# Laying x out by partition, loading it in eight groups, splitting the first piece of the adjacency matrix, and moving two waits to their first reader

## What is computed

```python
dn = de = diag(adj)
A  = adj with its diagonal set to zero
node_support = A @ h                                    # h is x
edge_output  = gru(node_support, h, edge weights)
for each of 3 heads:                                    # W is 128 x 128, a is 256 x 1
    hW = h @ W
    hp, hm = (A > 0) @ hW, (A < 0) @ hW
    e_plus  = leaky_relu([hp, hm] @ a);  e_minus = leaky_relu([hm, hp] @ a)
    att = softmax over a row of (e_plus where A > 0, e_minus where A < 0)
    edge_support += (att * A) @ hW
node_output = gru(edge_support / 3, h, node weights)
x = layernorm(x + de * edge_output + dn * node_output)
# second layer: a graph convolution with tanh(adj * adj), keeping 350 a row
x = layernorm(x + relu(new_adj @ (tanh(x @ W_proj + b) @ W_gcn) + b2))
```

## Time and profile before

| | us |
|---|---|
| median of three runs | 1399.0 (1397.55 to 1399.67) |
| the profiled execution, whole | 1400.07 |
| its span, first to last instruction | 1398.3 |
| TensorE busy in the span | 1349.2 (96%) |
| VectorE busy | 1027.8 (74%) |
| ScalarE busy | 960.9 (69%) |
| mean granted TensorE clock | 0.981 of full speed |

### The profile page before, as it was taken

One profiled execution on the slowest core, in us unless ns is written; L12 is line 12 of the kernel. 1 busy time (PEld: TensorE's weight loads), 2 busy tenths in 40 slices (PEclk: granted clock), 3 DMA queues, 4 the chain that ended last, 5 costly groups with the idle time before them and its releaser, 6 DMA issues.

```text
span 1398.3 us, 11293 instructions
## 1 busy us (share of the span) xinstructions
PE 1349.2 (96%) x3716; PEld 627.6 (45%) x3716; DVE 1027.8 (74%) x1327; ACT 960.9 (69%) x1086; POOL 88.6 (6%) x188
## 2 busy tenths in 40 slices
PE   7999999989999999999999999999997889999996
PEld 3544444355444444444444444444443444444455
DVE  3244333436699998999989999899957885678883
ACT  4355445317688988889888898898935654556663
POOL 0000001000010010100100100101002430000000
PEclk9899999999999999999999999999999989999998
DMA  9687888244324242242323324223062006888860
GB/s 365 248 281 270 283 281 272 109 108 159 136 91 145 84 150 103 92 164 91 136 90 121 136 90 153 104 90 121 0 280 96 30 16 213 300 299 302 301 222 17
DMA packets 49321, 228.91 MB, mean 164 GB/s; under 512 B 10536, under 2 KB 20456, under 8 KB 23528
## 3 DMA queue, kind: packets, MB, share of 16 engines
q1 hardware_dynamic: 46688, 225.55, 46.1%
q10 hardware_dynamic: 2568, 2.58, 0.5%
HBM read 223.82 MB, written 4.29 MB: 163 GB/s over the span
## 4 chain that ended last, share of the span: by engine, by line
PE 67%; DVE 6%; POOL 3%; issue 1%; ACT 1%; DMA 1%; SPq 0%; POOLq 0%; DVEq 0%
PE t_y_ps L1689 46%; PE t_y_ps L1262 11%; PE t_y_ps L1667 4%; PE rows_ps L1262 2%; DVE mask L1140 2%; PE t_es_ps L1660 1%; DMA pieces<-scratch_ns_t 1%; PE t_y_ps L1213 1%; ACT pieces L1007 1%; POOL h_newton L960 1%; POOL h_newton L956 1%; POOL h_newton L958 1%; POOL h_root L962 1%; PE t_y_ps L1215 0%; DVE x_sb L1121 0%
## 5 line engine op out<-in xcount | busy, mean ns | idle before, releaser
L1689 PE MATMUL t_y_ps<-mask,x_sb 128*128 128x512 f32 x1536 | 663.0, 592 | 0.3 <-DVE mask L1607 0.3
L1689 PEld LDWEIGHTS t_y_ps<-mask,x_sb 128*128 128x128 f32 x1536 | 290.1, 190 | 364.0 <-issue 342.9
L1607 DVE TENSOR_TENSOR mask<-mask 128x1536 f32<-128x1536 f32 x256 | 449.0, 1755 | 2.0 <-ACT mask L1491 2.0
L1491 ACT ACTIVATE mask<-mask,ones 128x1536 f32<-128x1536 f32 x256 | 399.7, 1562 | 0.0
L1484 ACT ACTIVATE mask<-mask,pieces 128x512 f32<-128x512 f32 x352 | 241.3, 712 | 31.7 <-PE t_y_ps L1689 28.4
L383 PE MATMUL ns_ps<-pieces,x_sb 128*128 128x512 f32 x512 | 232.2, 609 | 10.0 <-DMA pieces<-in_adj_c 7.7
L1593 DVE TENSOR_SCALAR mask<-mask,e_cols 128x512 f32<-128x512 f32 x416 | 188.1, 484 | 56.7 <-PE t_y_ps L1689 45.7
L1262 PE MATMUL t_y_ps<-mask 128*128 128x512 f32 (+1 forms) x448 | 182.1, 565 | 0.0
L383 PEld LDWEIGHTS ns_ps<-pieces,x_sb 128*128 128x128 f32 x512 | 96.9, 194 | 133.1 <-issue 132.6
L210 ACT ACTIVATE signs<-pieces 128x2048 fp8e4<-128x2048 f32 x64 | 122.3, 1911 | 30.9 <-DMA pieces<-in_adj_c 15.7
L1140 DVE SCALAR_TENSOR_TENSOR mask<-mask 128x2048 f32<-128x2048 f32 x64 | 142.7, 2284 | 0.0
(11 more groups left out here) (163 smaller groups left out, 662.8 us busy)
## 6 DMA issues: line engine op xcount, KB each, us to landing
mask<-in_adj_c SPq DMA_DIRECT2D x128, 1024.0 KB, 4.8
pieces<-in_adj_c SPq DMA_DIRECT2D x64, 1024.0 KB, 4.9
mask<-scratch_shifts SPq DMA_DIRECT2D x8, 1536.0 KB, 7.7
mask<-in_x_t SPq DMA_DIRECT2D x1, 2048.0 KB, 16.4
scratch_ns_t<-ns_sb ACTq DMA_DIRECT2D x8, 256.0 KB, 5.9
pieces<-in_x_t SPq DMA_DIRECT2D x8, 256.0 KB, 2.9
pieces<-scratch_ns_t SPq DMA_DIRECT2D x8, 256.0 KB, 3.9
out<-x_sb SPq DMA_DIRECT2D x7, 256.0 KB, 6.4
```

The lines of the kernel that those rows point to most:

```text
L1491: nc.scalar.activation(t, t, ACT.Exp, bias=ones[:, :], scale=-1.0).then_inc(exped, 1)
L1607: nc.vector.tensor_tensor(term(n), term(n), a, ALU.mult).then_inc(terms, 1)
L1689: mm = nc.tensor.matmul(y_ps[c % 2][h][:, :], x_sb[:, k, :], term(n)[:, h, :], start=k == 0, stop=k == NB - 1)
```

## The change

x is laid out ahead of the launch as in_x_p, [128, 32, 128], so that each partition's 32 tiles are next to each other and a group of four tiles is 2 KB. It is loaded in eight transfers of 256 KB, each issued just ahead of the piece that uses it (for n from 5 on behind the three waits of that piece), and each with a semaphore of its own. Piece 0 is loaded in four transfers of 256 KB (one tile for each partition, 2 KB next to each other), each with a semaphore, and TensorE waits for each just ahead of the matmul that reads it; VectorE and ScalarE wait for all four. The wait for `split` moves from the start of chunk 1 to pos_products(0), and the wait for `const_ready` to sum_e(0). Loads of slot 0 are counted one less (loads_of), since piece 0 no longer counts there. in_x goes.

```diff
--- before.py
+++ after.py
@@ -82,17 +82,21 @@
     engine.dma_start(pieces[:, n % RING, :, :], dram["adj_c"][c, :, g * PIECE:(g + 1) * PIECE, :]).then_inc(loaded[n % RING], 16)
 
 
+def loads_of(n):
+
+
+    return 16 * (n // RING + (1 if n % RING else 0))
+
+
 def wait_piece(engine, loaded, cleared, n):
 
     c, g = piece_of(n)
     if g == c:
         engine.wait_ge(cleared, CHUNK * (c + 1))
     else:
-        engine.wait_ge(loaded[n % RING], 16 * (n // RING + 1))
-
-
-X_SINGLE = 4
-X_REST = (slice((X_SINGLE + 1) * PIECE, NB), slice(0, PIECE))
+        engine.wait_ge(loaded[n % RING], loads_of(n))
+
+
 UV_AFTER = NPIECE - 1
 MASKS_FIRST = UV_AFTER + 3
 LAST_EARLY = 4
@@ -128,9 +132,10 @@
 
 
     w_ready, x_t_ready, const_ready = sem("a_w"), sem("a_x_t"), sem("a_const")
-    x_ready = [sem(f"a_x{n}") for n in range(X_SINGLE + 1)]
+    x_ready = [sem(f"a_x{n}") for n in range(NPIECE)]
     exps, parts_made, small = sem("a_exps"), sem("a_parts"), sem("a_small")
     loaded = [sem(f"a_loaded{s}") for s in range(RING)]
+    first_loaded = [sem(f"a_first_loaded{j}") for j in range(PIECE)]
     folded, folded_out, uv_done, uv_out, split = (sem("a_" + n) for n in ("folded", "folded_out", "uv_done", "uv_out", "split"))
     filled, cleared, masked, signed, ns_done, ns_out, pos_done, prod_out = (
         sem("a_" + n) for n in ("filled", "cleared", "masked", "signed", "ns_done", "ns_out", "pos_done", "prod_out"))
@@ -172,22 +177,25 @@
 
         @block.sync
         def _(sp):
-            x_rows = dram["x"].rearrange("(t p) f -> p t f", p=P)
-            for n in range(X_SINGLE):
-                tiles = slice((n + 1) * PIECE, (n + 2) * PIECE)
-                sp.dma_start(x_sb[:, tiles, :], x_rows[:, tiles, :]).then_inc(x_ready[n], 16)
-                load_piece(sp, dram, pieces, loaded, n)
-            for tiles in X_REST:
-                sp.dma_start(x_sb[:, tiles, :], x_rows[:, tiles, :]).then_inc(x_ready[X_SINGLE], 16)
-            for n in range(X_SINGLE, RING):
-                load_piece(sp, dram, pieces, loaded, n)
-            for n in range(RING, NPIECES):
+            for n in range(NPIECE):
+                tiles = slice((n + 1) % NPIECE * PIECE, ((n + 1) % NPIECE + 1) * PIECE)
+                if n >= RING:
+                    sp.wait_ge(masked, n - RING + 1)
+                    sp.wait_ge(signed, n - RING + 1)
+                    sp.wait_ge(ns_done, n - RING + 1)
+                sp.dma_start(x_sb[:, tiles, :], dram["x_p"][:, tiles, :]).then_inc(x_ready[n], 16)
+                if n:
+                    load_piece(sp, dram, pieces, loaded, n)
+                else:
+                    for j in range(PIECE):
+                        sp.dma_start(pieces[:, 0, j, :], dram["adj_c"][0, :, PIECE + j, :]).then_inc(first_loaded[j], 16)
+                if n == UV_AFTER:
+                    sp.dma_start(x_t, dram["x_t"]).then_inc(x_t_ready, 16)
+            for n in range(NPIECE, NPIECES):
                 sp.wait_ge(masked, n - RING + 1)
                 sp.wait_ge(signed, n - RING + 1)
                 sp.wait_ge(ns_done, n - RING + 1)
                 load_piece(sp, dram, pieces, loaded, n)
-                if n == UV_AFTER:
-                    sp.dma_start(x_t, dram["x_t"]).then_inc(x_t_ready, 16)
 
         @block.gpsimd
         def _(pool):
@@ -196,7 +204,7 @@
                 c, g = piece_of(n)
                 if g != c:
                     continue
-                pool.wait_ge(loaded[n % RING], 16 * (n // RING + 1))
+                pool.wait_ge(loaded[n % RING], loads_of(n))
                 for r in range(CHUNK):
                     one = pieces[:, n % RING, r, r * P:(r + 1) * P]
                     nc.gpsimd.tensor_tensor(one, one, off_diag[:, :], ALU.mult).then_inc(cleared, 1)
@@ -204,7 +212,8 @@
         @block.scalar
         def _(act):
             def count_below(n):
-                wait_piece(act, loaded, cleared, n)
+                if n:
+                    wait_piece(act, loaded, cleared, n)
                 if n:
                     act.wait_ge(signed, n)
                 nc.scalar.activation(signs[:, :], pieces[:, n % RING, :, :].rearrange("p k n -> p (k n)"), ACT.Relu, scale=-1.0, saturate=False,
@@ -225,7 +234,8 @@
                     act.wait_ge(e_sum, c - 1)
                 nc.scalar.copy(prod_sb[c % 2][:, :], pos_ps[c % 2][:, :]).then_inc(prod_out, 1)
 
-            act.wait_ge(loaded[0], 16)
+            for j in range(PIECE):
+                act.wait_ge(first_loaded[j], 16)
             act.dma_start(off_diag[:, :], dram["off_diag"]).then_inc(const_ready, 16)
             act.dma_start(w_t[:, :, :], dram["gat_W_t"].rearrange("h g f -> g h f")).then_inc(w_ready, 16)
             act.dma_start(a_sb[:, :, :], dram["gat_a"]).then_inc(w_ready, 16)
@@ -257,7 +267,11 @@
 
             def make_mask(n):
                 c, g = piece_of(n)
-                wait_piece(dve, loaded, cleared, n)
+                if n:
+                    wait_piece(dve, loaded, cleared, n)
+                else:
+                    for j in range(PIECE):
+                        dve.wait_ge(first_loaded[j], 16)
                 nc.vector.tensor_scalar(mask[:, c, g * PIECE:(g + 1) * PIECE, :], pieces[:, n % RING, :, :], 0.0, None, ALU.is_gt, saturate=False
                                         ).then_inc(masked, 1)
 
@@ -378,14 +392,19 @@
                 at = n % NPIECE
                 if at == 0 and c >= 2:
                     pe.wait_ge(ns_out, c - 1)
-                wait_piece(pe, loaded, cleared, n)
+                if n:
+                    wait_piece(pe, loaded, cleared, n)
                 for j in range(PIECE):
+                    if n == 0:
+                        pe.wait_ge(first_loaded[j], 16)
                     mm = nc.tensor.matmul(ns_ps[c % 2][:, :], x_sb[:, g * PIECE + j, :], pieces[:, n % RING, j, :], start=at == 0 and j == 0,
                                           stop=at == NPIECE - 1 and j == PIECE - 1)
                 mm.then_inc(ns_done, 1)
 
             def pos_products(c):
                 pe.wait_ge(masked, NPIECE * (c + 1))
+                if c == 0:
+                    pe.wait_ge(split, 2 * NPART - 1)
                 if c >= 2:
                     pe.wait_ge(prod_out, c - 1)
                 for k in range(NB):
@@ -398,6 +417,8 @@
                 pe.wait_ge(prod_out, c + 1)
                 if c:
                     pe.wait_ge(e_made, c)
+                else:
+                    pe.wait_ge(const_ready, 80)
                 nc.tensor.matmul(e_ps[0:NE, :], score[:, :], prod_sb[c % 2][:, :], start=True, stop=True).then_inc(e_sum, 1)
 
             def turn_e(c):
@@ -408,10 +429,7 @@
                 mm.then_inc(e_turned, 1)
 
             for n in range(UV_AFTER + 1):
-                if n < X_SINGLE:
-                    pe.wait_ge(x_ready[n], 16)
-                elif n == X_SINGLE:
-                    pe.wait_ge(x_ready[X_SINGLE], 16 * len(X_REST))
+                pe.wait_ge(x_ready[n], 16)
                 ns_products(n)
                 if n == UV_AFTER - 3:
                     pe.wait_ge(w_ready, 32)
@@ -424,9 +442,8 @@
                 last = nc.tensor.matmul(uv_ps[:, t * NUV:(t + 1) * NUV], x_t[:, t * P:(t + 1) * P], w6[:, :], start=True, stop=True)
             last.then_inc(uv_done, 1)
             for n in range(UV_AFTER + 1, NPIECE):
+                pe.wait_ge(x_ready[n], 16)
                 ns_products(n)
-            pe.wait_ge(const_ready, 80)
-            pe.wait_ge(split, 2 * NPART - 1)
             end = NCHUNK - 1
             for c in range(1, NCHUNK):
                 for g in range(NPIECE if c < end else LAST_EARLY):
@@ -2453,8 +2470,8 @@
 
     adj, x = np.asarray(inputs["adj"]), np.asarray(inputs["x"])
     lay = {
-        "x": x,
         "x_t": x.T,
+        "x_p": x.reshape(NB, P, H).transpose(1, 0, 2),
         "adj": adj,
 
         "adj_t": adj.reshape(NB, P, NB, P).transpose(0, 3, 2, 1).reshape(NB, P, N),
```

## The result

The changed kernel takes 1395.38 us (median of 12, 1392.82 to 1397.87) against 1399.34 for the kernel before (12 runs, 1397.55 to 1402.47): a ratio of 0.9972, interval 0.9964 to 0.9980, or 2.8 to 5.0 us less. Forecast were 5.6 us less and 1393.4 us, with a range of 1391.0 to 1396.4. The direction and the range held; about 1.6 us of the gain didn't come. Its profiled execution took 1397.11 us, with a span of 1395.4.

The account below looks back on a forecast made before the run. TensorE, busy 1349.2 of 1398.3 us, was taken as the bound, the DMA nearly even until uv. Gains of 2.3 + 1.2 - 0.2 + 2.26 made 5.6 us: 1399.0 to 1393.4, range 1391.0 to 1396.4.

Parts of the forecast that it names:

- Part 4, the waits: Ahead of chunk 1: moving the split wait wins its 2.26 us idle hole; no wait takes its place.
- the half-speed stretch: TensorE after uv, from chunk 1's start: 5.1 us at 1.2 GHz, taken as unchanged; bounds -2.5 and +2.5.
- Part 3, the order of x: Ahead of piece 4: it lands behind 256 KB of x instead of 1 MB, bringing uv 1.2 us forward.
- The ring waits: On SyncE, ahead of x groups 5, 6, 7 and 0: cost nothing, with 7.5 us of cover.
- Part 1, x by partition: x's DMA loads: 2 KB packets save 0.22 us in each of eight groups, 1.8 in all.
- Part 2, the split: Piece 0 in four transfers: TensorE starts 2.3 us earlier, at 4.2; all that lies behind pays 0.26.
- The straight line: DMA packet cost between 512 bytes (28 ns) and 8 KB (307 ns): 84 ns for 2 KB, 0.68 us a group.
- The DMA-bound case: Rival, first stage: 2 KB packets move at the 512-byte rate; 3.0 us won, 1396.0; chance 0.20.
- The clock comes back sooner: Rival, after uv: TensorE no longer pauses, up to 2.5 us more won, 1391; chance 0.08.
- Given back later: Rival, behind 248 us: a pause meets a clock fall it now misses, 1396 to 1399; chance 0.06.
- One transfer after another: Rival, piece 0's quarters: each takes its 2.9 us in turn, last lands 6.4 later, 1399.1; chance 0.05.
- The fall of the clock at a wait: Slower rival, pieces 2 to 7: short waits drop TensorE's clock; 1403.4 with 20 us more half speed; chance 0.04.

Follow-up runs that it names:

- one tile then three: Changed kernel with piece 0 in two transfers, the first tile and then the other three (6 KB packets): 1393.43 us, ratio 0.9964.
- the packed one: Changed kernel with piece 0's four quarters read from their own input, each quarter's 128 rows next to each other: 1396.01 us, ratio 0.9974.

## Why the prediction was right, and where it was off

**What bounds the kernel** was read rightly: what the first 60 us win arrives whole at the end.

**Part 4, the waits,** was right in the wait: the hole of 2.26 us is gone and nothing is late next. It was wrong in the price. The prediction took the half-speed stretch to last 5.1 us from the start of chunk 1, whenever that comes, and so the hole to be worth its full length. In the changed kernel's profile it does last 5.0 us from there, but by an earlier fall, which makes uv 1.1 us longer. The hole lay inside the stretch, and at equal stretches its removal is worth 1.2 to 1.3 us. The time measured for the waits alone, 0.4 to 3.1 us less, holds both numbers.

**Part 3, the order of x:** the wait ahead of piece 4 went in every kernel with x in eight groups. The ring waits cost nothing, as argued: SyncE issued x's sixth group at 14.55, and piece 4 landed at 21.8.

**Part 1, x by partition,** is a term of the wrong size. Landing of piece 7 was to be 1.8 us earlier; alone it was 1.0, and in the three kernels with x in eight groups and piece 0 whole 0.5 to 0.8 (31.15, 30.99 and 31.29 against 31.77). In the changed kernel the first x group took 3.3 us from issue to landing against 2.9, where 0.22 less was forecast; over all profiles it took 3.0 to 3.6 by partition and 2.9 to 3.1 with the old rows. That made the first matmul 0.6 late. Between 2 and 5 us the DMA moved 311 GB/s, 344 in the kernel before and 337 with x alone changed: I had priced the first microseconds by a rate from mid-stream. But half of what x alone fell short was lost behind piece 0, where each group saved 0.17 us and not 0.22.

**Part 2, the split,** is the other one. Priced at 0.26 us for what lies behind, it cost 1.5 on the kernel before, and on top of x by partition 0.4 to 1.5 (31.70, 31.83 and 32.51 with four quarters; 31.15, 30.99 and 31.29 with piece 0 whole). The straight line between packet sizes priced the bytes; there is a cost beyond them, which the distance of the rows doesn't explain, and which was seen in mid-stream as well. Whether it is the number of packets or of transfers, the runs don't tell: one tile and three has fewer of both.

Put together for the profiled executions: forecast at pos_products(0) 5.56 us, measured 3.01. uv began 1.55 late (piece 7 cleared at 33.4 instead of 32.0), and uv with pieces 8 and 9 took 57.76 - 37.05 = 20.7 us instead of 19.7. The first is the DMA's, parts 1 and 2. The second is part 4's: with stretches of the same 13.65 us at 1.2 GHz, half of the hole came back. As the two profiles have it the change gives 3.0 us, which would put the median at 1396.3, at the end of the range. The medians are 4.0 apart; the third us would be the clock's if the half-speed stretch is shorter in most executions of the changed kernel than in the one profiled (it is in its repetition, 10.2), but how long it lasts in the others isn't recorded. So the bound, the waits and the direction were read rightly, while that the time fell 1 us inside the range and not at its end is in part luck.

**The rivals.** The DMA-bound case was given 0.20 and 3.0 us, and its picture (slack gone, piece 7 and uv late) is what the trace shows, by a dearer split and a slower start and not by the 512-byte rate, at which x alone would have won nothing and not 1.0 us. Its median would have been 1396.0; the outcome lies between it and the forecast. "The clock comes back sooner" didn't happen in the profiled changed kernel (5.0 us after chunk 1 began) but did in others (3.0 with piece 0 whole, 3.3 with one tile then three). "Given back later" didn't happen. One transfer after another is ruled out: a second issued 0.46 us after the first lands 0.7 later, and the split pieces cost 0.4 to 1.5 us, not 6.4. The Trainium skill's fixed 2.0 us per DMA (DMA: Bandwidth & Descriptors, Anatomy of one DMA) is a fit to DMAs issued by GpSimd; on this queue, whose DMAs SyncE issues, whatever is fixed overlaps with its neighbours, while its advice to batch (Measured, under Bandwidth) points the right way: alone, the split lost time. The fall of the clock at a wait, named from the Trainium skill's TensorE: Matmul & The Clock Gate (HAM oscillation), did not happen in the changed kernel at 0.65 us nor in the waits alone at 2.38, and did at 2.56 in the split alone, where waits of 0.85 and 0.74 had gone before.

## What to carry to other kernels

Where the trace shows the DMA engines full and the compute engine's slack small, an earlier start is worth only what the last needed landing allows: follow the landings to the end of the full stretch before counting a start as won. If a first transfer is to be split, split it as little as the first consumer needs: one part for it and one for the rest kept the early start in three traces, though no time here shows the gain over no split at all. Take prices at the head of a queue from rows at the head of a queue. A wait at which everything piles up is cheap to move to its first reader; but where it lies in a stretch at half speed, count half of it, unless a run shows that the stretch gets shorter along with it.

## What the runs showed of the hardware

- uv and pieces 8 and 9 took 17.4, 19.1 or 20.7 us in the profiled executions without the hole (17.4 with piece 0 whole and with one tile then three; 19.1 with the waits alone, the repeated changed kernel and piece 3 split; 20.7 in the changed kernel and the packed one). The work is the same; the time at 1.2 GHz differs, 6.8, 10.2 and 13.7 us in the same order, and no length between them was seen. With the hole they took, it included, 20.3 us at 10.2 (the split alone) and 22.0 or 21.9 at 13.7 (before, x alone). The clock fell 2.6 to 5.2 us into uv. Steps of 1.7 us are as large as most parts of this change, so one profiled execution can't size such a part unless stretches of the same length are compared; ten executions give intervals of about 1.3 us to either side, which is barely enough.
- The clock fell from 2.4 to 1.2 GHz within the block of small matmuls (six columns) in all ten profiles that have it, while TensorE was busy without a pause (2.45 us at 1.00, then 8.40 at 0.50 in the changed kernel). In a mix with matmuls of 512 columns the clock stayed at 2.4 GHz in some executions (18 us at 1.00); in the two profiles where it had fallen it did not come back before the mix ended (20 us at 0.50). The two are some 11 us apart in the kernel's time.
- A median near 1400 hid five executions of twelve at 1388.3 to 1390.0, among them the fastest of all. Where times fall in two groups, the list says what the median can't.
